# A Mamba-and-experts kernel: normalisations and the first state moved to ScalarE, low halves and the gated rows' variance to GpSimd

## What is computed

```
for i in range(2):
    res = h
    h = layernorm(h, ln_w[i], ln_b[i])            # (x - mean) * rsqrt(var + eps) * w + b
    z, xBC, dt = split(h @ in_w.T)                # 512, 640, 8 columns
    dt = softplus(dt + dt_bias)
    xBC = silu(causal_conv4(xBC) + conv_b)
    x, B, C = split(xBC)                          # 8 heads of 64, state 64
    state_t = exp(dt*A) * state_{t-1} + dt * x_t B_t ;  y_t = state_t C_t + D x_t
    y = y * silu(z)
    y = y * rsqrt(mean(y*y) + eps) * rms_w
    h = y @ out_w.T + res
x1 = layernorm(x + h)
w, idx = top2(softmax, x1 @ gate_w + gate_b)
out = layernorm(x1 + sum_k w_k * expert_idx_k(x1))
```

## Time and profile before

| | |
|---|---|
| median of 3 runs | 1635.63 us (1634.18 to 1643.03) |
| the profiled execution: its own time, its span | 1643.5 us, 1641.6 us |
| ordinary units 1 to 8 | 113.4 to 499.6 us, 48.3 us each |
| routing units 9 to 14 | 499.6 to 876.7 us, 62.9 us each |
| last unit, closing step and plan | 876.7 to 972.4 us |
| expert part | 972.4 to 1591 us |
| closing sums and layer norm | 1591 to 1641 us |

### The profile page before, as it was taken

One profiled execution on the slowest core, in us unless ns is written; L12 is line 12 of the kernel. 1 busy time (PEld: TensorE's weight loads), 2 busy tenths in 40 slices (PEclk: granted clock), 3 DMA queues, 4 the chain that ended last, 5 costly groups with the idle time before them and its releaser, 6 DMA issues.

```text
span 1641.6 us, 40122 instructions
## 1 busy us (share of the span) xinstructions
PE 1353.8 (82%) x13198; PEld 1044.9 (64%) x13199; DVE 1160.7 (71%) x2658; ACT 741.4 (45%) x1682; POOL 780.7 (48%) x665
## 2 busy tenths in 40 slices
PE   2788888888887887887877529999999999999970
PEld 1355555556555554555544428999999999998960
DVE  4788988888988778688787656656565656565552
ACT  2554455554445424434432305445444444544443
POOL 1245555554654355455466626334132615072875
PEclk9799999999999888888887659999999999999995
DMA  4322323323332121330222132230313213123656
GB/s 138 103 65 78 116 93 112 97 70 103 103 116 73 58 97 53 98 93 30 97 93 106 60 128 90 89 111 29 106 32 109 83 58 106 32 80 98 103 104 147
DMA packets 97991, 145.88 MB, mean 89 GB/s; under 512 B 13504, under 2 KB 81856, under 8 KB 97792
## 3 DMA queue, kind: packets, MB, share of 16 engines
q1 hardware_dynamic: 79776, 98.51, 19.0%
q0 software_dynamic: 18144, 46.51, 10.9%
HBM read 103.19 MB, written 41.80 MB: 88 GB/s over the span
## 4 chain that ended last, share of the span: by engine, by line
PE 51%; DVE 16%; issue 15%; POOL 11%; ACT 2%; DMA 2%; SPq 1%; POOLq 1%; DVEq 0%; ACTq 0%
PE pe L814 11%; PE pa L814 11%; PE py L826 10%; DVE arena L1178 4%; PE pa L601 4%; PE py L690 3%; DVE arena L1215 3%; POOL arena L1855 3%; PE pm L721 3%; PE pa L593 3%; POOL arena L1784 2%; POOL arena L1774 1%; DVE arena L1223 1%; PE pt L792 1%; PE pz L696 1%
## 5 line engine op out<-in xcount | busy, mean ns | idle before, releaser
L814 PE MATMUL pe<-arena 128*128 128x128 f16 x3456 | 218.8, 219 | 6.4 <-issue 6.4
L814 PE MATMUL pa<-arena 128*128 128x128 f16 x3456 | 218.5, 219 | 0.0
L814 PEld LDWEIGHTS pe<-arena 128*128 128x128 f16 x3456 | 201.7, 97 | 13.3 <-issue 12.8
L826 PE MATMUL py<-arena 128*128 x1728 | 200.5, 273 | 2.8 <-DVE arena L1605 1.6
L814 PEld LDWEIGHTS pa<-arena 128*128 128x128 f16 x3456 | 200.9, 97 | 0.0
L1061 ACT ACTIVATE arena<-pe,arena 128x128 f32<-128x128 f32 x576 | 164.3, 373 | 79.9 <-PE pe L814 78.0
L1178 DVE SCALAR_TENSOR_TENSOR arena<-pa,arena 128x511 f32<-128x511 f32 (+2 forms) x240 | 178.2, 745 | 15.9 <-ACT arena L877 9.9
L1577 DVE SCALAR_TENSOR_TENSOR pm<-pa,arena 128x128 f32<-128x128 f32 x288 | 81.7, 352 | 139.3 <-ACT arena L1061 130.2
L826 PEld LDWEIGHTS py<-arena 128*128 128x128 f16 x1728 | 165.6, 98 | 21.7 <-issue 3.6
L1784 POOL TENSOR_TENSOR arena<-arena 128x512 f32<-128x512 f32 x64 | 81.3, 1270 | 202.2 <-DVE arena L1242 201.9
L721 PE MATMUL pm<-arena 128*128 128x256 f16 x768 | 114.3, 308 | 49.4 <-DVE arena L1151 49.4
(11 more groups left out here) (219 smaller groups left out, 2480.6 us busy)
## 6 DMA issues: line engine op xcount, KB each, us to landing
arena<-step_rows SPq DMA_DIRECT2D x64, 512.0 KB, 4.5
arena<-in_w_exp POOLq DMA_DIRECT2D x32, 768.0 KB, 4.8
arena<-queue SPq DMA_DIRECT2D x75, 129.5 KB
answer<-arena SPq DMA_DIRECT2D x72, 128.0 KB
arena<-in_x SPq DMA_DIRECT2D x16, 512.0 KB, 5.8
answer<-zeros SPq DMA_DIRECT2D x10, 512.0 KB, 4.7
arena<-h SPq DMA_DIRECT2D x9, 512.0 KB, 5.2
h<-arena SPq DMA_DIRECT2D x8, 512.0 KB, 2.9
```

Of the source, the lines that this page charges most:

```text
L814: ins = pe.matmul(bank[:, f * P:(f + 1) * P], w_split[:, p, hl, d * 2 * FF + col:d * 2 * FF + col + P], x[:, r, d, :], start=(n == 0), sto ...
L826: ins = pe.matmul(py[:, 0:D], a[:, b, f, :], part(p, hl, W1N + f * D, D), start=(half == 0 and n == 0), stop=(half == 1 and n == len(passe ...
```

## The change

ScalarE takes over `ln_apply` and the applying of x1 (now `x1_apply`), as an Identity activation with scale rs and bias -mean*rs for each of the four tiles, and the copy of chunk 0's new state (`first_state`). GpSimd takes over `u_low` and the variance of the gated rows (now inside `end`); it also makes the bias, a second small product behind each power -0.5, for which VectorE makes -mean. The scale 1/512 of the gated rows' variance goes into the Square activation. The steps of every engine are cut into smaller functions, but PE's order stays, and that of the steps that stay on their engine. The new steps stand here: `first_state` on ACT between `steps` and `conv_silu(c4)`; `x1_apply` on ACT after `b_rows`, ahead of `chunk_a(c[2])`; `ln_apply` on ACT after `z_silu(1)`; both `u_low` on POOL after the products of the next unit's chunk 0 and ahead of the last two scatters.

```
@@ ScalarE @@
+            def ln_apply(w, wq):
+                e.wait_ge(ln_rs, w + 1)
+                for k in range(NK):
+                    ins = e.activation(hln[:, wq, k, :], hln[:, wq, k, :], ACT.Identity, scale=rs[:, k:k + 1],
+                                       bias=nb[:, k:k + 1])
+                ins.then_inc(ln_done, 1)
+
+            def x1_apply(st):
+                wq = 1 - st.q
+                e.wait_ge(r_rs, st.u - NB)
...
+                for k in range(NK):
+                    ins = e.activation(x1b[:, wq, k, 0:D], ob[:, wq, k, :], ACT.Identity, scale=rrs[:, k:k + 1],
+                                       bias=rnb[:, k:k + 1])
+                ins.then_inc(x1_ready, 1)
+
+            def first_state(c):
+                e.wait_ge(z_full, c.u6 + 1)
+                e.activation(state[0:DS, 0].rearrange("p h d -> p (h d)"), pz[0:DS, :], ACT.Copy).then_inc(z_free, 1)
...
                     steps(st)
                 if st.first:
                     high_weights(1)
+                first_state(c[0])
                 if s1:
                     conv_silu(st, "c4")
                 chunk_a(c[1])
                 chunk_c(c[0])
+                squares(c[0])
...
                     conv_silu(st, "c1")
                     b_rows(st)
+                if s3:
+                    x1_apply(st)
                 chunk_a(c[2])
...
                 chunk_c(c[2])
+                squares(c[2])
                 if s1:
                     z_silu(st, 1)
+                    ln_apply(st.u + 2, st.q)
                 chunk_d(c[2])
@@ VectorE @@
+                at_least(dve, ln_rs, w)
+                dve.tensor_scalar(nm, mv[:, :, 0], -1.0, None, ALU.mult)
                 dve.tensor_scalar(ve, mv[:, :, 1], EPS, None, ALU.add).then_inc(ln_var, 1)
-
-            def ln_apply(w, wq):
-                dve.wait_ge(ln_rs, w + 1)
-                for k in range(NK):
-                    ins = dve.tensor_scalar(hln[:, wq, k, :], hln[:, wq, k, :], mv[:, k, 0:1], rs[:, k:k + 1],
-                                            ALU.subtract, ALU.mult)
-                ins.then_inc(ln_done, 1)
...
-                if k < NK - 1:
-                    dve.wait_ge(z_full, c.u6 + 2 * k + 1)
-                    new = pz[0:DS].rearrange("p (h d) -> p h d", h=NH)
-                    if k == 0:
-                        dve.tensor_copy(state[0:DS, 0], new).then_inc(z_free, 1)
...
+                at_least(dve, r_rs, st.u - NB - 1)
+                dve.tensor_scalar(rnm, rmv[:, :, 0], -1.0, None, ALU.mult)
                 dve.tensor_scalar(rve, rmv[:, :, 1], EPS, None, ALU.add).then_inc(r_var, 1)
...
-                if not st.first:
-                    end_a(st)
...
-                if s3:
-                    s3_apply(st)
...
-                if s1:
-                    ln_apply(st.u + 2, st.q)
...
-                if s1:
-                    u_lows(st)
@@ GpSimd @@
+            def u_low(w, wq, st, name):
+
+                (bank, before), d = st.fill(name), int(name[2])
+                pool.wait_ge(a_free[bank], before + 1)
+                pool.tensor_tensor(uT[:, wq, 1, d, :], uf[:, d, :], uT[:, wq, 0, d, :], ALU.subtract
+                                   ).then_inc(ul_ready, 1)
+
             def rsqrt_ln(w):
                 pool.wait_ge(ln_var, w + 1)
-                pool.tensor_tensor(rs, ve, half_neg[:, :], ALU.pow).then_inc(ln_rs, 1)
+                at_least(pool, ln_done, w)
+                link(pool.tensor_tensor(rs, ve, half_neg[:, :], ALU.pow), ln_pow, w)
+                pool.tensor_tensor(nb, nm, rs, ALU.mult).then_inc(ln_rs, 1)
 
             def end(st):
-                pool.wait_ge(sve_ready, st.u)
+                pool.wait_ge(ss_ready, 4 * st.u)
+                pool.sem_inc(hop, 1)
+                link(pool.tensor_scalar(sve, ss[:, 1 - st.q], 1.0, EPS, ALU.mult, ALU.add), sve_ready, st.u - 1)
                 pool.tensor_tensor(srs, sve, half_neg[:, :], ALU.pow).then_inc(srs_ready, 1)
...
                 gated(c[3])
                 if not st.last:
-                    operands(c[4])
-                scatter_before(st, 6, 8)
+                    x_dt(c[4])
+                    x_w(c[4])
+                    x_d(c[4])
+                    u_low(st.u + 2, st.q, st, "ln0")
+                    u_low(st.u + 2, st.q, st, "ln1")
+                scatter_before(st, 6, 7)
+                scatter_before(st, 7, 8)
```

More of the change, by code:

```diff
@@ L1006, in body @@
                 else:
-                    for n in range(1, 4):
-                        high_parts(n)
+                    high_parts(1)
+                    high_parts(2)
+                    high_parts(3)
             def prologue(st):
@@ L1017, in prologue @@
                 conv_silu(st, "c4")
-                for c, then in zip(CONV_ORDER[1:], CONV_ORDER[2:]):
-                    conv_first(st, then)
-                    conv_silu(st, c)
+                conv_first(st, "c1")
+                conv_silu(st, "c0")
+                conv_first(st, "c2")
+                conv_silu(st, "c1")
+                conv_first(st, "c3")
+                conv_silu(st, "c2")
                 z_silu(st, 0)
-                conv_silu(st, CONV_ORDER[-1])
+                conv_silu(st, "c3")
+                ln_apply(1, 1)
                 z_silu(st, 1)
@@ L1034, in epilogue @@
                 gap_tanh(st)
+            ln_apply(0, 0)
             e.wait_ge(params, 16 * N_PARAMS)
@@ L1136, in wait_fill @@
                 return bank, before
-            def u_low(w, wq, d, bank, fills):
-                dve.wait_ge(a_free[bank], fills)
-                dve.tensor_tensor(uT[:, wq, 1, d, :], uf[:, d, :], uT[:, wq, 0, d, :], ALU.subtract).then_inc(ul_ready, 1)
-            def u_lows(st):
-                for d in range(KD):
-                    bank, before = st.fill(f"ln{d}")
-                    u_low(st.u + 2, st.q, d, bank, before + 1)
             def g_low(c):
@@ L1406, in prologue @@
                 ch1 = Chain(dve, c_dve2, S1_LINKS, 0)
-                for d in range(KD):
-                    bank, before = st.fill(f"ln{d}")
-                    u_low(0, 0, d, bank, before + 1)
                 dt_first(st)
@@ L1413, in prologue @@
                 taps(st, "c4", ch1)
-                ln_apply(1, 1)
                 taps(st, "c0", ch1)
                 weigh(st)
-                for c in CONV_ORDER[2:]:
-                    taps(st, c, ch1)
+                taps(st, "c1", ch1)
+                taps(st, "c2", ch1)
+                taps(st, "c3", ch1)
                 ch1.close()
                 scan(Chunk(st, NK))
-                for d in range(KD):
-                    bank, before = st.fill(f"ln{d}n")
-                    u_low(1, 1, d, bank, before + 1)
                 chunk_mix(Chunk(st, NK))
             def epilogue(st):
-                end_a(st)
                 end_b(st)
@@ L1708, in load_weights, with first_weights @@
                     pool.dma_start(w_raw[:, a:b], w_exp[e, :, a:b]).then_inc(w_raw_in, 16)
+            def first_weights():
+                for s in range(2):
+                    pool.wait_ge(a_free[s], LAST_HB)
+                load_weights(0)
             def split(e):
@@ L1791, in body @@
                 if st.last:
-                    for s in range(2):
-                        pool.wait_ge(a_free[s], LAST_HB)
-                    load_weights(0)
+                    first_weights()
                 gated(c[0])
-                operands(c[1])
+                x_dt(c[1])
+                x_w(c[1])
+                x_d(c[1])
+                old_state(c[1])
                 if not st.first and not st.s3:
```

211 lines of the change are left out of this document (144 added, 67 removed).

## The result

The changed kernel takes 1710.7 us (median of 4 runs, 1709.5 to 1711.3), the kernel before 1637.7 (1634.2 to 1643.0): a ratio of 1.044 (95% interval 1.041 to 1.047). Slower, as forecast, but by 73 us and not by 23.5. All medians here are of fast executions; one of the six of the run with spare matmuls in the kernel before was slow (1716.0 us at a granted clock of 0.82) and is left out. The profiled execution has a span of 1709.0 us, against 1641.6.

The account below looks back on a forecast made before the run. A ring through VectorE, POOL, TensorE and ScalarE was taken to set the pace. 23.5 us (13 clock, 9.5 ordinary, 1 start), +1 routing, -1 end, added to 1635.6, gave 1659 us; 8-in-10 range 1633 to 1675.

Parts of the forecast that it names:

- What the gap does to TensorE's clock: Ordinary units, ahead of chunk 0's turn: half clock behind a 2.8 us gap, six of eight units, 2.2 us each: 13 us.
- First state: Head of ordinary units: copy on ScalarE makes chunk 1's `chunk_b2` 0.2 us later, spending the 0.9 us VectorE saves.
- Power and product ahead of the gating: Ordinary units, normalising: wait and small product on GpSimd add 0.28 us; the product of -mean adds 0.1.
- Low halves and variance: End of ordinary units: the second low half on GpSimd adds 0.47 us, variance behind it 0.13.
- Routing units: Six units together +1 us (range -5 to +8); a clock fall at the first gap replaces the one behind 2.89 us.
- the ring: Loop setting the pace: VectorE mid-unit, POOL's gating, TensorE's chain, ScalarE's `ln_out`, low halves, dt fill; edits count by its change.
- unit 0 and the first fills: Start, ahead of the ordinary units: +1 us, as ScalarE comes late in unit 0 anyway.
- the last unit and the closing step: End of the kernel: -3.5 us for `s3_apply`, +1.5 for late scatters and variance, +1 in the closing step, together -1.
- B: Rival: the clock holds behind the new gaps, same sum without the 13 us: 1646 us (1638 to 1650), chance 0.25.
- C: Rival: ScalarE's wait costs nothing, because the load precedes the copy or `xs` has slack: 1633 us (1628 to 1640), chance 0.12.
- D: Rival: VectorE is the pace throughout; all its relief back gives 1566 us, half gives 1600; chance 0.10.
- E: Rival: longer gap, and the clock falls in routing units too without replacing the old fall: 1680 us, chance 0.08.

Follow-up runs that it names:

- held kernels: Kernel before and changed kernel, each with spare matmuls fitted to TensorE's gaps to hold its clock up: 1622.3 us and 1630.5 us.
- held kernel before: Kernel before plus spare matmuls in TensorE's gaps, more of them in routing units: 1622.3 us, ratio 0.988.
- held changed one: Changed kernel, all parts moved, plus the same spare matmuls and 12 more ahead of the turn of chunk 0: 1630.5 us, ratio 0.993.

## Why the prediction was wrong

**The step that failed is "What the gap does to TensorE's clock".** I had put one fall into six of eight ordinary units at 2.2 us (13 us), and none into the routing units, since the new fall would replace the one behind 2.89 us. Measured against the held kernels, with the 0.8 us of spare matmuls that fill no gap taken off the changed one (49.7 - 0.8 = 48.9): a changed ordinary unit loses 52.9 - 48.9 = 4.0 us to the clock, one before 48.3 - 47.5 = 0.8, so 3.2 times 8 = 26 us, twice my term. Most of it is at the place that I had named: the fall came in all eight units and cost 2.8 us in each (15.47 against 12.70 from y of chunk 0 to y of chunk 1), not 2.2 in six. A changed routing unit loses 66.7 - 58.8 = 7.9 us, one before 62.9 - 61.1 = 1.8, so 6.1 times 6 = 36 us, where I had nothing. For routing units the sign was right for the first two stretches (one fall instead of another, and c1-c2 gains 3.3 us) but I stopped there: the same units wait again ahead of the turn of chunk 2 and behind it, and these waits had grown: the gap ahead of that turn from 1.3 to 1.4 us to 1.6 to 1.8 in four of the five full routing units, through power and product, the tail through low halves and variance behind the scatters. Behind them the logits' fill, which took 2.0 to 2.1 us in three of the five before and 2.4 and 3.4 in the others, takes 2.9 to 3.6 us in each.

I had also read a limit between 2.61 and 2.74 us out of three gaps, where the same trace had shorter gaps with half clock behind them. In units 1 and 2 of the kernel before, TensorE waits equally long for the same turn of chunk 3, and the first is at half clock:

```profile
157.49 1.11 PE L705 MATMUL pt<-ident,arena 128*128 128x128 f32 x4 [1.51 <-POOL arena L1784]
205.54 0.65 PE L705 MATMUL pt<-ident,arena 128*128 128x128 f32 x4 [1.51 <-POOL arena L1784]
```

The split has a weakness in the routing units: the held kernel before is at a clock of 0.96 there and the held changed one at 0.99. In unit 11 of the former a fill of z still takes 2.61 us instead of 1.46, behind a wait of 2.03 us for VectorE that no spare matmul fills:

```profile
642.05 0.66 PE L615 MATMUL pa<-ident,arena 128*128 128x128 f32 x4 [2.03 <-DVE arena L1194]
642.55 2.61 PE L601 MATMUL pa<-arena 128*128 128x512 f16 x6
```

So its stretch from chunk 1 to chunk 2 (19.1 against 18.0) is longer by clock and not by fillers, and part of what I call the change's gain there is clock. The five spare matmuls ahead of chunk 0's output product stand in the held routing units too (13.51 us from y of chunk 0 to y of chunk 1); what they cost a whole unit there is not separated.

**The waits, term by term, in ordinary units with the clock at 1.00.** First state: I had 0.2 us at chunk 1's `chunk_b2`, measured 0.26 (49.70 - 48.63, less 0.81 of spare matmuls); the slack absorbed nearly all of the 2.45 us, as forecast. Power and product ahead of the gating: 0.28 and 0.1, measured 0.42 (47.91 - 47.49). Low halves and variance: 0.47 + 0.13, measured 0.72 (48.63 - 47.91). Together 1.4 instead of 1.2, times 8 = 11 us instead of 9.5. These terms were sound.

**Routing units.** I had +1 us for six; against the held kernel before they gain: 6 times (58.8 - 61.1) = -14, some of it clock, as said. VectorE's relief does reach the ring there: with the normalisations alone moved and both kernels at 0.96, a unit gains 1.8 us. Clock and waits of both kinds of unit come to 26 + 36 + 11 - 14 = 59 of the 60 us.

**Ahead of and behind these units.** I had +1 us for unit 0 and the first fills and -1 for the last unit and the closing step; measured 2.3 and 5.0. The last unit takes 46.0 us instead of 45.8, so the 3.5 us that I took off did not come. Where the rest of the 5.0 lies was not traced; with spare matmuls in both kernels it is 2.6.

**What held.** The load 0.65 us after the state product's end (0.6); the x copy 2.5 us later against y; the gap 2.84 (2.8); half clock behind it; VectorE's wait for y 3.74 to 3.83 (3.8); power and product 1.3; low halves 1.16; the normalise on ScalarE 0.59 each, hidden. Of the rivals, B falls: the clock does not hold. C falls, and its way out, the load ahead of the copy, recovers 37 of the 73 us. D falls for the kernel as changed, yet a piece of it is true: in routing units with spare matmuls the relief of VectorE is worth some 2 us. E was the nearest (1680, the clock falls in routing units too), though its gap was no longer than reckoned, and I had priced it far too low and given it 0.08.

**What stays open.** In the routing units, why the clock is back at 0.86 with low halves on VectorE while the gap ahead of the turn of chunk 2 is still 1.7 us, and only at 0.83 with the layer norm there and the gap at 1.37: the fall cannot be put down to that one gap, and these runs do not separate what else takes part. Each clock is also from one profiled execution of a kernel whose four runs spread over 18 to 20 us. Nor was it tried whether a few fillers in the tail of routing units alone would do.

## What to carry to other kernels

Price an added wait on TensorE twice: by its length, and by what the matmuls behind it cost at half clock; count every place in a unit where TensorE already waits, since here a few tenths more there went along with more half clock. A look at the granted clock by stage comes before any talk of which engine is busy. Before moving work between engines, try spare matmuls in TensorE's gaps: they show within one run what the clock costs, and may be worth keeping. Check in each kernel's timeline that they stand in a gap: where none is, they cost their own length (0.81 us a unit here), and a comparison takes that for an effect of the change. And ask what an activation from another table set finds in its way when something is put ahead of it.

## What the runs showed of the hardware that I had not expected

- Gaps far under the 2.74 us of the earlier trace rows lie ahead of half clock: 1.41 us (the fill behind it 2.33 instead of 1.47) and 1.77 us (the turn itself 1.11 instead of 0.65). In the kernel before, behind the same wait of 1.51 us, one turn took 1.11 us and another 0.65. Behind 2.61 us the next product was fast. The length of one gap does not tell whether the clock falls.
- Ordinary units of the same instructions differ by 2 us: in the changed kernel the stretch from y of chunk 2 to y of chunk 3 takes 10.5 to 11.2 us in four of them and 12.7 to 13.0 in the other four, and with the clock held 11.0 to 11.3 in all (10.7 to 10.9 in the kernel before).
- Some 490 added matmuls of 0.18 to 0.20 us took 20 us off the kernel before, and 670 took 80 off the changed one.
- A product of 128x4 on GpSimd takes 0.20 us, where a power of the same shape takes 1.02.
